# A fused transformer layer on one core: attention written out and reordered, expert rows added to DRAM

## What is computed

```python
h = _L0_tok_ref(log_dt, inv_A_real, A_imag, B_ri, x, 256)      # Vandermonde sum, (8, 256, 256)
h = jnp.concatenate([h, txt], axis=1)                          # (8, 768, 256)
h = h + attn(_layernorm(h), Wq, Wk, Wv, Wo)
h = h + ffn(_layernorm(h), Wr, br, W1, b1, W2, b2)

# attn: q, k rotated (rotary), softmax(q k^T / 8) v, heads joined, @ Wo
# ffn:
logits = xf @ Wr + br
topk_w, topk_idx = jax.lax.top_k(logits, 2)
topk_w = jax.nn.softmax(topk_w, axis=-1)
gate = jnp.sum(jax.nn.one_hot(topk_idx, 8) * topk_w[..., None], axis=1)
h = jax.nn.relu(jnp.einsum('th,ehf->etf', xf, W1) + b1[:, None, :])
y = jnp.einsum('etf,efh->eth', h, W2) + b2[:, None, :]
out = jnp.einsum('te,eth->th', gate, y)
```

## Time and profile before

| | us |
|---|---|
| median of 3 runs | 2702.7 (2696.3 to 2704.5) |
| the profiled execution | 2709.1 |
| its span, first to last instruction | 2707.3 |
| vandermonde and the start of attention | 184 |
| attention, from the first maximum | 1652 |
| route | 279 |
| experts | 457 |
| combine | 135 |

### The profile page before, as it was taken

The page is one execution under the profiler, slowest core; times in us unless marked ns, Lnnn a source line. Parts: engine busy times, 40 slices in busy tenths (PEclk is TensorE's granted clock), DMA queues, the critical chain, the costliest instruction groups (busy, mean ns, idle before and its releaser), DMA issues. The chain is left out here.

```text
span 2707.3 us, 59046 instructions
## 1 busy us (share of the span) xinstructions
PE 2210.2 (82%) x20292; PEld 1180.7 (44%) x20293; DVE 1780.5 (66%) x2903; ACT 1052.7 (39%) x2156; POOL 808.8 (30%) x752
## 2 busy tenths in 40 slices
PE   0458998998998998998998999886996699999900
PEld 0433343343343343443343343335885466666600
DVE  8438888888888878978978988962545222222223
ACT  1025555555555645655655555531111122222200
POOL 0042523523523523433433342200344000000076
PEclk6578999999999999999999999998997799999955
DMA  2222342342342333333333324316774211111144
GB/s 43 56 78 50 96 112 68 94 106 73 95 104 72 98 90 87 98 82 94 94 82 91 89 81 98 86 49 202 238 253 146 68 62 61 62 62 62 55 133 146
DMA packets 216852, 258.20 MB, mean 95 GB/s; under 512 B 57248, under 2 KB 181664, under 8 KB 216608
## 3 DMA queue, kind: packets, MB, share of 16 engines
q1 hardware_dynamic: 186016, 209.84, 29.0%
q0 software_dynamic: 9216, 25.18, 2.8%
q10 hardware_dynamic: 21376, 19.93, 2.2%
HBM read 105.40 MB, written 61.34 MB: 62 GB/s over the span
## 5 line engine op out<-in xcount | busy, mean ns | idle before, releaser
L631 ACT ACTIVATE a_prob<-ps_s,a_nmax 128x768 f32<-128x768 f32 x768 | 692.4, 902 | 743.2 <-DVE a_nmax L749 721.3
L749 DVE TENSOR_REDUCE a_nmax<-ps_s 128x1 f32<-128x768 f32 x768 | 718.2, 935 | 238.4 <-PE ps_s L561 231.9
L561 PE MATMUL ps_s<-a_kT,a_qT 64*128 64x384 f32 x3072 | 677.5, 535 | 129.4 <-ACT a_prob L631 102.7
L755 DVE STREAM_TRANSPOSE a_probT<-a_prob 128x768 f32<-128x768 f32 x768 | 735.9, 962 | 0.0
L568 PE MATMUL ps_o<-a_probT,a_vrep 32*64 32x384 f32 x12288 | 574.3, 500 | 38.7 <-ACT a_xnext L619 15.6
L561 PEld LDWEIGHTS ps_s<-a_kT,a_qT 64*128 64x128 f32 x3072 | 241.3, 188 | 538.2 <-ACT a_prob L631 359.2
L568 PEld LDWEIGHTS ps_o<-a_probT,a_vrep 32*64 32x64 f32 x12288 | 248.1, 134 | 334.7 <-issue 138.6
L695 POOL TENSOR_TENSOR a_o<-a_o,a_invrow 128x1536 f32<-128x1536 f32 x32 | 110.1, 3442 | 811.1 <-ACT a_o L639 811.1
L444 POOL TENSOR_TENSOR a_prod<-a_raw,a_table 128x384 f32<-128x384 f32 x312 | 302.3, 1001 | 31.7 <-ACT a_raw L623 24.5
L1355 POOL DMA_INDIRECT c_yg<-ys_d,c_idx x96 | 93.2, 971 | 497.3 <-DVE c_idx L1322 468.4
L1275 DVE TENSOR_TENSOR e_h<-ps_eh,eb 128x512 f32<-128x512 f32 x104 | 71.9, 692 | 234.6 <-PE ps_eh L1205 233.5
(11 more groups left out here) (202 smaller groups left out, 1574.0 us busy)
## 6 DMA issues: line engine op xcount, KB each, us to landing
a_qT<-a_qp SPq DMA_DIRECT2D x512, 96.0 KB, 3.7
a_vrep<-a_vraw SPq DMA_DIRECT2D x512, 48.0 KB, 2.0
a_invrow<-inv_d SPq DMA_DIRECT2D x64, 384.0 KB, 4.9
oT_d<-a_o SPq DMA_DIRECT2D x32, 768.0 KB, 3.3
r_oT<-oT_d SPq DMA_DIRECT2D x192, 128.0 KB
e_x<-xs_d SPq DMA_DIRECT2D x104, 128.0 KB, 2.0
ys_d<-e_y ACTq DMA_DIRECT2D x104, 128.0 KB, 1.7
ew<-in_L_ffn_W_dram SPq DMA_DIRECT2D x16, 512.0 KB
```

What stands on the lines that cost most here:

```text
L561: last = pe.matmul(S[:, s % 2, r, 0:HALF], qT[rows, par, 2 * hp + c, P * t:P * t + P], kT[rows, par, :], start=True, stop=True)
L631: act.activation(prob[:, s % RING, :].rearrange("p (r k) -> p r k", r=2), S[:, s % 2, :, 0:HALF], ACT.Exp, bias=nmax[:, s % RING:s % RING ...
L749: v.tensor_reduce(nmax[:, s % RING:s % RING + 1], S[:, s % 2, :, 0:HALF], AX.XY, ALU.max, negate=True).then_inc(max_ready, 1)
L755: v.transpose(turned(par, s), prob[:, s % RING, :]).then_inc(t_ready, 1)
```

## The change

Three parts.

Attention has no loop any more: all batches are written out with constants. VectorE does the maxima of two steps and then two transposes: `TURN_AT` turns the slices s-3 and s-2 in the odd steps from 3 on, and four in step 23. The jobs move to the odd steps 17 to 23, up to two a step, and are shared out anew: 4, 7, 8 and 7 for the four heads instead of 7, 6, 6 and 7. The statistics are cut into six pieces and stand in steps 17, 19 and 21 of the last two heads, one batch earlier. The inverse is made in step 17 instead of 2, and SyncE moves it behind the values instead of ahead of the queries. GpSimd rotates both halves of the keys in the fourth head. The copy of the normalised input (`xnow`, `xnext`) becomes one buffer `xT`.

In routing each scattered row is 8 words longer and carries its token's number, its two experts and their weights. The sum `h1` is also stored to a DRAM tensor `acc_d`, one batch at a time.

In the experts VectorE reads token numbers and weight for each tile (`gates`), scales the tile by the weight, and GpSimd adds its 128 rows to `acc_d` by an indirect DMA that adds; each waits for the one before to land. `combine` is gone; eight copies move `acc_d` to the output.

```diff
@@ attention
-    JOBS = [Q_JOBS + N_JOBS, Q_JOBS + K_JOBS[:2], Q_JOBS + K_JOBS[2:], Q_JOBS + V_JOBS]
+    JOBS = [Q_JOBS, Q_JOBS + N_JOBS, Q_JOBS + K_JOBS, Q_JOBS + V_JOBS]
...
-    JOB_AT = {0: [], 4: [17, 18, 20, 22], 6: [17, 18, 20, 21, 23, 24], 7: [17, 18, 19, 20, 22, 23, 24]}
+    JOB_AT = {0: [], 4: [17, 21, 23, 23], 7: [17, 19, 19, 21, 21, 23, 23], 8: [17, 17, 19, 19, 21, 21, 23, 23]}
...
-    TURN_AT = {s: [s - 2] for s in range(2, STEPS - 1)}
-    TURN_AT[STEPS - 1] = [STEPS - 3, STEPS - 2]
+    TURN_AT = {s: [s - 3, s - 2] for s in range(3, STEPS, 2)}
+    TURN_AT[STEPS - 1] += [STEPS - 2, STEPS - 1]
...
-    INV_AT, NORM_AT = 2, 8
+    INV_AT = 17
+    STATS_AT = [(KV - 2, 17), (KV - 2, 19), (KV - 2, 21), (KV - 1, 17), (KV - 1, 19), (KV - 1, 21)]
...
-            for g in range(KV):
-                iteration(0, g)
-            with eng.Fori(1, NB - 1) as b:
+            for b in range(NB):
                 for g in range(KV):
                     iteration(b, g)
-            for g in range(KV):
-                iteration(NB - 1, g)
...
-                    if not first_it(i):
-                        move_inv(i - 1)
                     if not last_it(i):
                         move_q((g + 1) % 2, i + 1)
...
                     move_v(b, g)
                     if not first_it(i):
+                        move_inv(i - 1)
                         store(i - 1)
...
-                    if g >= 2 and not last_batch(b):
-                        c = g - 2
-                        rotate(pool, "k", c, b * 2 + (2 + c), scratch, job_no(b, g - 1, len(Q_JOBS) + 2), (k_in[1], (b * 2 + 2) * (K_MOVES * 16)))
+                    if g == KV - 1 and not last_batch(b):
+                        for c in range(2):
+                            rotate(pool, "k", c, b * 2 + (2 + c), scratch, job_no(b, 2, len(Q_JOBS) + 2 * c + 2), (k_in[1], (b * 2 + 2) * (K_MOVES * 16)))
@@ route
+                def store(b):
+                    act.wait_ge(h1_ready, b * TT + (TT + 3))
+                    act.dma_start(acc_d[bass.ds(b * SEQ, SEQ), :].rearrange("(t p) d -> p t d", p=P), h1[:, b]).then_inc(h_stored, 16)
...
-                    v.tensor_copy(gate[:, b, 0, :], gr[:])
-                    v.tensor_tensor(gate[:, b, 1, :], ex[:], gr[:], ALU.mult)
+                    v.tensor_copy(xn[:, q, :, D].bitcast(I32), tok_i[:, b, :])
+                    v.tensor_copy(xn[:, q, :, D + 1:D + 1 + TOPK], top[:])
+                    v.tensor_copy(xn[:, q, :, D + 3], gr[:])
+                    v.tensor_tensor(xn[:, q, :, D + 4], ex[:], gr[:], ALU.mult)
@@ experts
-                def store(j, n):
-                    act.wait_ge(y_ready, j + 1)
-                    act.dma_start(ys_d[j], y[:, n, :]).then_inc(stored[n], 16)
...
+                def tile(j, n):
+                    hold(pool, y_ready, j + 1)
+                    if not (isinstance(j, int) and j == 0):
+                        hold(pool, added, j * 16)
+                    pool.indirect_dma_start(out=acc_d, out_offset=bass.IndirectOffsetOnAxis(ap=row_i[:, n:n + 1], axis=0),
+                                            in_=y[:, n, :], in_offset=None, compute_op=ALU.add).then_inc(added, 16)
...
+                    hold(v, bias_ready, j + 1)
+                    v.tensor_scalar(y[:, n, :], y[:, n, :], gate[:, n:n + 1], None, ALU.mult).then_inc(y_ready, 1)
+
+                def gates(j, n):
+
+                    hold(v, x_in[n], (j >> 2) * 16 + 16)
+                    if not (isinstance(j, int) and j < RING):
+                        hold(v, added, (j - RING + 1) * 16)
+                    v.tensor_copy(row_i[:, n:n + 1], x[:, n, D:D + 1].bitcast(U32))
+                    v.tensor_tensor(is_it[:, n, :], x[:, n, D + 1:D + 1 + TOPK], held_by[:, bass.ds(j, 1)].to_broadcast([P, TOPK]), ALU.is_equal).then_inc(gate_dve, 1)
+                    hold(v, gate_dve, j * 2 + 1)
+                    v.tensor_tensor(share[:, n, :], is_it[:, n, :], x[:, n, D + 3:D + 3 + TOPK], ALU.mult).then_inc(gate_dve, 1)
+                    hold(v, gate_dve, j * 2 + 2)
+                    v.tensor_tensor(gate[:, n:n + 1], share[:, n, 0:1], share[:, n, 1:2], ALU.add).then_inc(gate_ready, 1)
...
-                loop(v, tile, renumber)
+                loop(v, tile)
...
+        with nc.Block() as block:
+            @block.sync
+            def _(sp):
+                copied = sem("copied")
+                for b in range(NB):
+                    sp.dma_start(out[b].rearrange("(p t) d -> p (t d)", p=P), acc_d[SEQ * b:SEQ * b + SEQ, :].rearrange("(p t) d -> p (t d)", p=P)).then_inc(copied, 16)
+                sp.wait_ge(copied, 16 * NB)
```

More of the change, by code:

```diff
@@ L35 @@
 NT = TOK * TOPK // P + NE
+DX = D + 8
 F32 = mybir.dt.float32
@@ L639, in copy_o, with copies @@
                     act.activation(o[:, :, :, q, :], O[:, q, 0:HALF].rearrange("p (h t s) -> p h t s", h=2, t=TT), ACT.Copy).then_inc(o_out, 1)
-                def late(b, g):
-                    if first_it(b * KV + g):
-                        return []
-                    rows = jobs(b, g - 1) if g else JOBS[KV - 1]
-                    before = (b, g - 1, b * KV + g - 1) if g else (None, KV - 1, b * KV - 1)
-                    return [(n, jobs_before(b, g, n), rows[n], before) for n in range(len(rows)) if JOB_AT[len(rows)][n] == STEPS - 1]
+                def copies(b, g, s):
+                    i = b * KV + g
+                    for n, (job, c, h) in jobs_at(b, g, s):
+                        free = None
+                        if job == "q" and h == 0:
+                            free = part["q"], i * (2 * LINKS) + (2 + c + 1) * LINKS
+                        if job == "k" and h == 0:
+                            free = part["k"], b * (2 * LINKS) + (c + 1) * LINKS
+                        if (job, c) == ("v", 0):
+                            free = v_in, i * (V_MOVES * 16) + V_MOVES * 16
+                        evacuate(O[:, n % NQ], job_no(b, g, n), job, c, h, free)
                 def iteration(b, g):
@@ L766, in iteration @@
                         maxima(i, s)
-                        if s == 0 and not first_it(i):
-                            turn(i - 1, 1 - par, STEPS - 1)
                         for n in TURN_AT.get(s, ()):
@@ L772, in iteration @@
                             invert(i - 1, 1 - par)
[L773 to L774 removed]
+                        for n, at in stats_at(b, g, s):
+                            stats(n, at)
                 def drain():
[L777 removed]
                     invert(NIT - 1, 1)
[L780 removed]
+                for at in range(6):
                     stats(0, at)
@@ L1152, in wait, with loop @@
                 eng.wait_ge(s, value)
-        where, moved, past = (sb(f"e_{x}", [P, NB * TOPK * TT]) for x in ("where", "moved", "past"))
-        pos_dve = sem("e_pos_dve")
-        def loop(eng, tile, between=None):
+        def loop(eng, tile):
             for n in range(RING):
                 tile(n, n)
-            if between:
-                between()
             with eng.Fori(1, NT // RING - 1) as k:
@@ L1258, in tile, with _ @@
                     relu_h(j, q)
-                    if not (isinstance(j, int) and j < 2):
-                        store(j - 2, (n - 2) % RING)
                 copy_x(0, 0)
                 loop(act, tile)
-                for n in (2, 3):
-                    store(NT - RING + n, n)
-                for n in range(RING):
-                    act.wait_ge(stored[n], NT // RING * 16)
+            @block.gpsimd
+            def _(pool):
+                def tile(j, n):
[4 more added lines that the diff above has]
+                                            in_=y[:, n, :], in_offset=None, compute_op=ALU.add).then_inc(added, 16)
+                loop(pool, tile)
+                pool.wait_ge(added, NT * 16)
             @block.vector
```

237 lines of the change are left out of this document (82 added, 155 removed).

## The result

The changed kernel takes 2552.9 us (median; 2534.5 to 2558.8) against 2699.5 for the kernel before: a ratio of 0.944, 95% interval 0.940 to 0.949. That is 147 us less, where 216 were forecast. The time lies inside the range and 66 us above the forecast, on the way to the first rival. Of the later runs, two have one execution of four that was far slower than the rest (2682.6 us of the plain scatter, 12094.8 of the eight slots); the ratios leave it out, and the medians of the three others are 2494.1 and 2529.3.

A forecast was written before the change was run, and what follows sets the result against it. PE and VectorE bound attention, PE the experts, serial indirect loads the combine. Attention -124, routing +5, experts -5 and +10, end -102 gave -216 from 2707.3: 2491, less 4.6 for the median 2487 us; range 2440 to 2600.

The forecast's parts named there:

- the first rival: Experts: the adds set the pace, period between 4.4 and 5.2 us, at 5.2 +88 us, 2575 us; chance 0.26.
- Pair of steps: Attention, values phase: two maxima then two transposes bring two steps to 3.61 us instead of 3.85.
- Batches: Attention: 188 us a batch, from 185.3 by the compute engines and 188.6 by the queues; 205.3 on average before.
- the ring: Attention: closed cycle of value copies, inverse, GpSimd scaling, rotation and query copies; 46.2 us an iteration, 3.8 more in fourth head.
- drain: Attention, last batch's end: last transposes come earlier, -6 us.
- Routing: Routing stage: an added 768 KB store per batch, longer scattered rows and small VectorE copies cost +5 us.
- VectorE's extra work in the experts: Experts: four tiny instructions and a 128x256 scaling per tile cost +0.1 us a tile, +10 us in all.
- The adds as hidden: Experts: GpSimd's chained adds to DRAM have a period of 4.3 us, just what a tile takes, so they cost nothing.
- The bounds: Experts, period of the adds: lower 3.33 us from a plain scatter, upper 5.2 if reading the sum's rows adds in series.
- The prediction's signs: Experts: add period above 4.4 us, and PE's idle naming y or VectorE's naming the add, would show the first rival.
- End: After the last bias: combine goes, last scaling and add, block end and copies take its place; 137 to 35 us, -102.
- the copies at the pace of a lone store: End: the eight final DRAM-to-DRAM copies would take 20 us at that pace; the forecast took 29.

The follow-up runs named there:

- the plain scatter: Changed kernel with a plain scatter in place of the indirect add, the sum of expert rows left out: 2496.5 us, 0.923 of the kernel before.
- the eight slots: Changed kernel with eight slots instead of four for rows, weights and results of the experts: 2530.2 us, 0.935 of the kernel before.
- attention alone: Kernel before with only the attention of the changed kernel, everything else as before: 2588.7 us, 0.960 of the kernel before.
- the run by expert: Changed kernel, an add waiting for the one two places before, and the one just before only if the expert changes: 2486.0 us, ratio 0.921.
- without loads: Changed kernel with the loads of the expert rows left out from the fifth tile on: 2519.1 us, 0.932 of the kernel before.
- new experts alone: Attention of the kernel before with routing, experts and end of the changed kernel: 2666.7 us, 0.987 of the kernel before.
- the run with the early inverse: Changed kernel with the inverse made in step 3 instead of 17 and moved ahead of the value copies: 2580.5 us, 0.957 of the kernel before.

## Why the prediction was off by 66 us

- **Pair of steps** (3.61 forecast, 3.61 measured) right. **Batches** 188 forecast, 186.8 in the profile of the changed kernel and 187.5 with attention alone. By heads 45.2, 45.4, 47.1 and 49.1 to 50.8 (nine traces) for 44.1, 45.2, 47.7 and 48.3. The fourth is longer by the ring, whose 50.0 in that head the sum had spread over the batch instead of setting it against that head alone. The first two heads take less than the ring's 46.2, so it does not bind there, and that 188 came so near is in part luck.
- **First batch** -3 for -7, **last** -17 for -7, **drain** 0 or 1 for -6 (31 us from the last maximum to routing's first transfer before, 32 now). Why the last batch gained more than forecast I did not look into. In the first iteration the statistics of the second batch meet GpSimd's rotations: 53.7 us, where the kernel before takes 50.9.
- **Attention** as a whole -112 by the runs, -124 forecast. By the profiled spans it is -121.5 (2707.3 to 2585.8, attention alone); the rest is that the profiled execution of before lies 8 us above the median of its runs here (2709.1, 2700.9), of which the forecast had allowed for less.
- **Routing** +5 forecast, +6 and +7 in two traces, but +5 also with the old routing behind the new attention; its own price lies between 0 and 7, not resolved further.
- **VectorE's extra work in the experts** (+10 forecast) costs nothing: tiles take 4.23 us with it, in the run by expert (435.8 us for 103), and 4.24 without it, in the kernel before (440.6, less the 4 of the renumbering).
- **The adds as hidden** is the step that failed. The bounds were right, 3.33 to 5.2, and so was the rival; the value was not. I took the middle, 4.3, because it lay between the ends, and it happened to be the length of a tile. The generation of 1.55 us was in no row; nor was the landing 3.5 to 3.9 us behind the start (without loads; 2.4 for the plain scatter). How much of that is the reading of the sum's rows, from which the upper bound was made, no run sets apart. The undisturbed chain has 4.5 and the locked one 5.0, and both are above the tile. Against forecast, experts are 48 us longer (53.5 for 5, new experts alone). By rival 1's own price a mean period of 503/103 = 4.88 costs 55 us. The prediction's signs said the same before any experiment: VectorE's waits name the add, and the adds start over 4.4 us apart. That the time still lies in the stated range is because the range took in most of rival 1, not because the sum had this step right.
- **End** -94 for -102: copies 22 for 29 (that pieces of 6 KB would bring them near the fast end was an estimate, and no run sets the size of the pieces apart), but two terms were too small, the queue of three adds behind the last bias (11 for 5) and the end of the block with the last landing (10 for 1). The 20 us that the prediction gives for the copies at the pace of a lone store don't follow from its row, by which eight stores of 4.0 us would take 32; the sum doesn't use them.

48 + 8 + 2 for the rest and 12 for attention are 70, against 66 measured (2487 to 2553). VectorE's work, the added scaling in it, did not lengthen the generation of the adds: it is 1.55 us beside that work and in the last three adds, where VectorE is idle. The gathers of the earlier trace rows don't settle it: both lie beside VectorE's work, and one takes 0.95 us, the other 1.22. In the whole combine the 12 gathers over 1 us all lie there, and so do some twenty of 0.95. And VectorE runs scalar_tensor_tensor there, not the tensor_scalar of the change:

```profile
2590.46 2.46 DVE L1328 SCALAR_TENSOR_TENSOR c_part<-c_yg,c_gt,h 128x256 f32<-128x256 f32 x6 [17.45 <-DMA c_yg<-ys_d,c_idx]
```

The lengthening that a run does show is in attention, where the prediction did not look, and it falls on VectorE: beside GpSimd's arithmetic, in the run with the early inverse, VectorE's tensor_tensor instructions on 6 numbers for each partition took 0.85 to 0.92 us instead of 0.17, and the tensor_scalar ones 0.92 to 2.84.

## What to carry to other kernels

A chain of dependent transfers has a period that must be measured before it is called hidden; when its lower bound is below the stage's pace and its upper bound above, the middle is no estimate, and the chance of the rival is near one half. If it can't be hidden, ask which links really depend on each other: here a table of waits took 67 us off, although few adds ran side by side with it. And look at what a blocked queue locks in step with: one wait more, which moved a load by one microsecond, gave half of that.

## What was not expected of the hardware

- An indirect DMA that adds takes 1.55 us to generate for 128 rows of 1 KB, for 0.96 without the add, and 3.5 to 3.9 us from its start to its landing with no load beside it (up to 4.5 in the changed kernel), for 2.4. A bounds check with rows beyond it left the generation at 1.55.
- A load of 132 KB issued 1.0 to 1.5 us behind the start of such an add made its period 0.4 us longer (4.97 for 4.54); issued at its start or over 2 us behind, less than 0.1 (4.53 to 4.58).
- A chain of small dependent VectorE instructions beside GpSimd's arithmetic went at GpSimd's pace, one for one: 0.92 us each for 0.17. VectorE's maxima and transposes beside the same work kept their time (two maxima 1.82 us in both, two transposes 1.83).
- Copying 6.3 MB from DRAM to DRAM took 21.9 us, 287 GB/s counted once.
